# Convolution stage: GpSimd folds four of nine term slots into four others, TensorE sums five, and the low half of the products comes in two pieces

## The chip, the core and the metric

The kernel runs on one core of a Trainium2 chip. The metric is device time in microseconds (us), the median of several executions; lower is better. Five engines work side by side, each in the order of its own queue: TensorE (PE in the profile; PEld is its weight load), VectorE (DVE), ScalarE (ACT), GpSimd (POOL) and SyncE (SP), which only issues DMAs here. They meet through semaphores.

## What is computed

A two-block network on x of 8 x 256 x 512 (batch, rows, columns) with a context of the same shape. The change touches only the first part of the first block, the long convolution:

```
k_ = k.reshape(B, H, head_dim, L)        # k and v are ctx, q is layernorm(x)
kv = jnp.einsum('bhil,bhjl->bijhl', k_, v_)
y = irfft(rfft(kv, n=2 * L) * rfft(ssm_kernel, n=2 * L))[..., :L]
out = y + kv * D
out = jnp.einsum('bijhl,bhil->bjhl', out, q_)
x = x + jnp.tanh(g_xattn[0]) * out
```

with 8 batches, 32 heads, 8 rows per head and L = 512. For each head and each pair (i, j) of rows the product of two context rows is convolved along its 512 columns with the head's filter, weighted with a row of the normalised x, and summed over i. Everything after it (mixture of experts, linear attention, soft mixture of experts) stays as it is.

## The kernel before, in words

The convolution is done by conv_stage (line 141) as multiplication with a Toeplitz matrix. Since k and v are the same tensor, only the 36 pairs with i <= j are made (PAIRS). The stage runs in 16 steps (STEPS, index s) of two heads each, and each step in 4 blocks of 128 columns (KD, index m). Per step:

- VectorE, pairs(s) (lines 340 to 354): the products of context rows, 2304 elements in each of 128 partitions, in f32, as two instructions of 2048 and 256 elements. Both inputs of both lie in SBUF.
- ScalarE, split(s) (line 307): prod_hi, the products rounded to f16.
- GpSimd (line 274): prod_lo, what the rounding left over, also f16, in one instruction.
- TensorE, convolve(s, m) (line 451): for the two heads and the blocks up to m three matmuls each, high by high, high by low and low by high; 6, 12, 18 and 24 matmuls for m = 0 to 3. The result lies in a ring of three PSUM places. It waits for the Toeplitz tile of its step (toep_loaded) and for the low half (lo_done).
- VectorE, weigh(s, m) (lines 380 to 383): four multiplications of the PSUM result with q_e, into the f32 tile terms. Its 72 places of 16 elements are nine slots (SLOTS_T) of 128 elements; 8 results (j) by 16 lie in each slot. terms has three buffers (M_BUFS).
- TensorE, add_up(n) with n = 4s + m (line 468): nine transposes with accumulation in PSUM add up the nine slots and turn them back.
- VectorE, add_rows(s) (line 392): tanh(gate) times the sum, plus x.
- SyncE (lines 253 to 258): the Toeplitz load of step s + 2 (two buffers), 8 stores of step s, 8 loads of x for step s + 2, in this order, in one queue.

TensorE's order is convolve(n), then add_up(n - 2). VectorE's order in step s is weigh(s,0), weigh(s,1), weigh(s,2), add_rows(s-1), pairs(s+2), weigh(s,3) (lines 419 to 431). In steps 1 to 4 further transposes of the second half of the inputs lie between them ("turn", in steps 1 to 4 after m = 1 and m = 3), and in steps 2 and 3 the LayerNorm of the second half ("normalise" and "scale"). weigh(n) waits until add_up(n - 3) has freed its buffer, and convolve(n) until weigh of the unit three places earlier has freed its place in the ring.

Of the kernel before, what the change touches and what calls it, by code (L numbers as in the profile page):

```python
# [14 lines left out]
ALU = mybir.AluOpType  # L15
AX = mybir.AxisListType

P = 128
# [3 lines left out]
KD = D // P  # L22
# [16 lines left out]
def opener(nc, stack):  # L39

    def sb(name, shape, dt=F32):
        return stack.enter_context(nc.sbuf_tensor(name, shape, dt))

    def ps(name, shape, dt=F32):
        return stack.enter_context(nc.psum_tensor(name, shape, dt))

    def sem(name):
        return nc.alloc_semaphore(name)
    return sb, ps, sem
# [68 lines left out]
STEPS = SSM_H // 2  # L118
GSTEPS = STEPS // 2
PAIRED = 2 * B * PAIRS  # L120
SLOTS_T = 9
RUN = 8 * SLOTS_T
WRAP = SSM_I + 4


def spread(a, *dims):

    return bass.AP(tensor=a.tensor, offset=a.offset, ap=[a.ap[0], *([s, n] for s, n in dims)])
# [12 lines left out]
def conv_stage(nc, k, x, ctx, ssm_reversed, ssm_d, g_xattn, g_ffn, ssm_split, x1):  # L141
# [5 lines left out]
    with phase(nc) as st:  # L147
        sb, ps, sem = opener(nc, st)
# [5 lines left out]
        T_BUFS, M_BUFS, RING = 2, 3, 3  # L154
        toep = sb("toep", [P, T_BUFS, 2, 2, D], F16)
        prod = sb("prod", [P, 2, PAIRED * KD])
        prod_hi, prod_lo = (sb(f"prod_{n}", [P, 2, KD, 2, B * PAIRS], F16) for n in ("hi", "lo"))
        terms = sb("terms", [P, M_BUFS, RUN, 2 * B])
# [10 lines left out]
        toep_loaded = [sem(f"toep_loaded{u}") for u in range(T_BUFS)]  # L169
        res_loaded, stored = [sem(f"res_loaded{u}") for u in range(2)], [sem(f"stored{u}") for u in range(2)]  # L170
        prod_done, hi_done, lo_done = sem("prod_done"), sem("prod_hi_done"), sem("prod_lo_done")
        conv_done, weighed, summed, added = sem("conv_done"), sem("weighed"), sem("summed"), sem("x_added")
        block = st.enter_context(nc.Block())

        x_t, c_t = (a.rearrange("b (e g r) d -> g e r b d", e=2, g=2) for a in (x, ctx))
# [44 lines left out]
        @block.sync  # L220
        def _(sp):
            def load(t, g, u):
                for e in range(2):
                    src = (c_t if t == "c" else x_t)[g, e, :, u * 4:u * 4 + 4, :]
                    sp.dma_start(rows[t][e * 64:e * 64 + 64, u * 4:u * 4 + 4, :], src).then_inc(loaded[t][u], 16)

            def load_res(s):
                if s >= 2:
                    sp.wait_ge(added, s - 1)
                for j in range(SSM_I):  # L230
                    sp.dma_start(res[j * 16:j * 16 + 16, s % 2, :], x_s[s, j]).then_inc(res_loaded[s % 2], 16)

            def load_toeplitz(s):
                sp.wait_ge(conv_done, (s - T_BUFS + 1) * KD)
                toeplitz(sp, s)

            def store(s):
                sp.wait_ge(added, s + 1)
                for j in range(SSM_I):
                    sp.dma_start(x1_s[s, j], gated[j * 16:j * 16 + 16, s % 2, :]).then_inc(stored[s % 2], 16)  # L240

            for t in "cq":
                for u in range(2):
                    load(t, 0, u)
            load_res(0)
            load_res(1)
            for u in range(2):
                sp.wait_ge(turned["c"], 2 * u + 2)
                load("c", 1, u)
            for u in range(2):  # L250
                sp.wait_ge(normed, 4 * u + 4)
                load("q", 1, u)
            for s in range(STEPS):
                if s + T_BUFS < STEPS:
                    load_toeplitz(s + T_BUFS)
                store(s)
                if s + 2 < STEPS:
                    load_res(s + 2)
            for u in range(2):
                sp.wait_ge(stored[u], STEPS // 2 * 128)  # L260

        @block.gpsimd
        def _(pool):
            nc.gpsimd.memset(k.ident[:, :], 0.0).then_inc(ident_zeroed, 1)
            pool.wait_ge(ident_zeroed, 1)
            nc.gpsimd.affine_select(out=k.ident[:, :], in_=k.ident[:, :], compare_op=ALU.not_equal, fill=1.0,
                                    base=0, pattern=[[-1, P]], channel_multiplier=1).then_inc(ident_ready, 1)
            nc.gpsimd.memset(terms[:, :, :, :], 0.0).then_inc(zeroed, 1)
            for s in range(STEPS):
                u = s % 2  # L270
                pool.wait_ge(hi_done, s + 1)
                if s >= 2:
                    pool.wait_ge(conv_done, (s - 1) * KD)
                nc.gpsimd.tensor_tensor(prod_lo[:, u].rearrange("p k e r -> p (k e r)"), prod[:, u, :],  # L274
                                        prod_hi[:, u].rearrange("p k e r -> p (k e r)"), ALU.subtract).then_inc(lo_done, 1)

        @block.scalar
        def _(act):
# [49 lines left out]
        def _(dve):  # L328
# [11 lines left out]
            def pairs(s):  # L340

                u = s % 2
                if s >= 2:
                    dve.wait_ge(lo_done, s - 1)
                if s == 0:
                    dve.wait_ge(out_act, 4)
                    dve.wait_ge(out_dve, 4)
                if s == GSTEPS:
                    dve.wait_ge(out_act, turns["c", 1, 3] + 1)
                c = c_e[:, s].rearrange("p k e b i -> p (k e b) i")  # L350
                dst = prod[:, u, :].rearrange("p (r n) -> p r n", n=PAIRS)
                nc.vector.tensor_tensor(spread(dst, (PAIRS, 64), (8, 4), (1, 8)), spread(c, (WRAP, 64), (0, 4), (1, 8)),
                                        spread(c, (WRAP, 64), (1, 4), (1, 8)), ALU.mult)
                nc.vector.tensor_tensor(dst[:, :, 32:PAIRS], c[:, :, 0:4], c[:, :, 4:8], ALU.mult).then_inc(prod_done, 1)
# [79 lines left out]
        @block.tensor  # L434
        def _(pe):
            pe.wait_ge(ident_ready, 1)

            def turn(unit):
                t, g, n = unit
                wait_free(pe, unit)  # L440
                if t == "c":
                    pe.wait_ge(loaded["c"][n // 2], (g + 1) * 32)
                else:
                    pe.wait_ge(normed, g * 8 + n * 2 + 2)
                for half in range(2):
                    for b in range(KD):
                        row = rows["c"][:, 2 * n + half, :] if t == "c" else xn[:, 2 * (n % 2) + half, :]
                        last = nc.tensor.transpose(ring[:, bank(unit), half, b * P:(b + 1) * P], row[:, b * P:(b + 1) * P], k.ident[:, :])
                last.then_inc(turned[t], 1)

            def convolve(s, m):
                unit, u = ("conv", s, m), s % T_BUFS
                wait_free(pe, unit)
                if m == 0:
                    pe.wait_ge(toep_loaded[u], (s // T_BUFS + 1) * 16)
                    pe.wait_ge(lo_done, s + 1)
                for e in range(2):
                    out = ring[:, bank(unit)].rearrange("p h c -> p (h c)")[:, D + (e - 1) * B * PAIRS:D + e * B * PAIRS]
                    for n in range(m + 1):
                        t = D - P - (m - n) * P  # L460
                        w_hi, w_lo = (toep[:, u, e, q, t:t + P] for q in range(2))
                        hi, lo = (a[:, s % 2, n, e, :] for a in (prod_hi, prod_lo))
                        nc.tensor.matmul(out, w_hi, hi, start=(n == 0), stop=False)  # L463
                        nc.tensor.matmul(out, w_hi, lo, start=False, stop=False)  # L464
                        last = nc.tensor.matmul(out, w_lo, hi, start=False, stop=(n == m))  # L465
                last.then_inc(conv_done, 1)

            def add_up(n):

                s, m = divmod(n, KD)  # L470
                pe.wait_ge(weighed, n + 1)
                if m == 0 and s >= 2:
                    pe.wait_ge(added, s - 1)
                out = total[:, s % 2, m * P:(m + 1) * P]
                for o in range(SLOTS_T):
                    last = nc.tensor.matmul(out, terms[:, n % M_BUFS, o * 8:o * 8 + 8].rearrange("p j n -> p (j n)"), k.ident[:, :],
                                            is_transpose=True, start=(o == 0), stop=(o == SLOTS_T - 1))
                last.then_inc(summed, 1)

            for unit in units:  # L480
                if unit[0] != "conv":
                    turn(unit)
                    continue
                convolve(*unit[1:])
                n = unit[1] * KD + unit[2]
                if n >= 2:
                    add_up(n - 2)
            add_up(STEPS * KD - 2)
            add_up(STEPS * KD - 1)


# [1736 lines left out]
```

## Time and profile before

| | us |
|---|---|
| median of three executions | 2036.13 (2035.11 to 2039.6) |
| the profiled execution, whole | 2038.1 |
| its span, first to last instruction | 2036.3 |
| convolution stage, first matmul of step 0 to the end of the last add_rows | 51.1 to 265.0 |

| engine over the whole span | busy us | share |
|---|---|---|
| PE | 1699.5 | 83% |
| DVE | 1141.6 | 56% |
| ACT | 716.2 | 35% |
| POOL | 419.4 | 21% |

All times are counted from the start of the span. A busy PE is not PE at its peak. In brackets behind a row stands how long the engine had been idle before it, and what ended that; "issue" means that the profile shows nothing that it waited for. A DMA's time in the timeline is the time of issuing it, not that of the transfer. A repetition "x9" stands for nine instructions in a row.

### The profile page before, as it was taken

The page shows a single profiled execution, that of the slowest core. Times are in us where ns is not written, and L with a number is a line of the kernel's source. Part 1 is how long each engine was busy: PE and PEld are TensorE (multiplying, and loading weights), DVE is VectorE, ACT ScalarE, POOL GpSimd, SP SyncE. Part 2 cuts the span into 40 slices and gives each one's busy share as a digit, 9 for nine tenths or more (in the row PEclk, how much of TensorE's full clock was granted, in tenths as well). Part 3 has the DMA queues.
Part 4 walks back from the last instruction along what each step waited for, and adds up shares of the span by engine and source line. Part 5 has one row for each costly group of instructions (what it writes and reads, how often), then busy time and mean ns, then how long its engine had stood idle before and what let it go on. Part 6 is the DMA issues. An engine that isn't in the chain of part 4 may idle for free. (4 is left out here: it accounts for less than half of the span.)

```text
span 2036.3 us, 29066 instructions
## 1 busy us (share of the span) xinstructions
PE 1699.5 (83%) x10248; PEld 1006.8 (49%) x10249; DVE 1141.6 (56%) x2234; ACT 716.2 (35%) x1366; POOL 419.4 (21%) x324
## 2 busy tenths in 40 slices
PE   2989948999279999588988736798989898989898
PEld 2778823444146666344544413454545454545454
DVE  4978843332643333576868646646465655556463
ACT  2322113333222222242333225735454443535352
POOL 1323303333411110233222113501010101010100
PEclk6999979999689999789999868899999899999999
DMA  8222233333422222433020052200000000000000
GB/s 179 62 74 86 86 119 107 119 119 99 134 68 84 82 82 68 185 104 103 13 92 21 11 176 66 90 1 32 1 32 0 31 0 31 0 31 0 21 13 20
DMA packets 78734, 134.52 MB, mean 66 GB/s; under 512 B 6626, under 2 KB 31202, under 8 KB 78514
## 3 DMA queue, kind: packets, MB, share of 16 engines
q1 hardware_dynamic: 71488, 113.45, 17.4%
q0 software_dynamic: 5680, 18.62, 3.2%
q10 hardware_dynamic: 1474, 1.21, 0.2%
q8 instruction: 59, 0.97, 0.2%
q14 instruction: 33, 0.27, 0.0%
HBM read 101.98 MB, written 31.28 MB: 65 GB/s over the span
## 5 line engine op out<-in xcount | busy, mean ns | idle before, releaser
L2041 PE MATMUL s_ring<-w_mu_hi,s_xt_hi 128*128 128x512 f16 x256 | 104.7, 409 | 45.7 <-DVE s_xt_lo L1948 45.7
L1953 DVE TENSOR_REDUCE s_top<-s_lg 128x1 f32<-128x512 f32 x64 | 43.8, 685 | 130.5 <-ACT s_lg L1855 130.5
L463 PE MATMUL ring<-prod_hi,toep 128*128 128x288 f16 x320 | 93.0, 291 | 18.2 <-DVE terms L383 10.1
L274 POOL TENSOR_TENSOR prod_lo<-prod,prod_hi 128x2304 f16<-128x2304 f32 x16 | 73.2, 4576 | 166.9 <-ACT prod_hi L307 156.6
L2025 DVE TENSOR_TENSOR s_g_lo<-s_ring,s_g_hi 128x512 f16<-128x512 f32 x64 | 43.4, 689 | 109.9 <-ACT s_g_hi L1897 109.9
L2042 PE MATMUL s_ring<-w_mu_lo,s_xt_hi 128*128 128x512 f16 x256 | 104.4, 408 | 0.0
L2043 PE MATMUL s_ring<-w_mu_hi,s_xt_lo 128*128 128x512 f16 x256 | 103.8, 405 | 0.0
L1800 POOL TENSOR_TENSOR s_h_lo<-s_h,s_h_hi 128x512 f16<-128x512 f32 x32 | 36.9, 1154 | 311.7 <-DVE s_h_hi L2022 311.7
L1794 POOL TENSOR_TENSOR s_xln<-s_xln,s_gamma 128x512 f32<-128x512 f32 x16 | 21.7, 1376 | 372.2 <-DVE s_xln L1934 372.2
L2041 PE MATMUL s_ring<-w_w_hi,s_xt_hi 128*128 128x512 f16 x256 | 98.0, 383 | 0.0
L2042 PE MATMUL s_ring<-w_w_lo,s_xt_hi 128*128 128x512 f16 x256 | 98.0, 383 | 0.0
L2043 PE MATMUL s_ring<-w_w_hi,s_xt_lo 128*128 128x512 f16 x256 | 97.8, 382 | 0.0
L2041 PE MATMUL s_acc<-w_w_hi,s_g_hi 128*128 128x512 f16 x256 | 97.1, 379 | 0.0
L2042 PE MATMUL s_acc<-w_w_lo,s_g_hi 128*128 128x512 f16 x256 | 97.0, 379 | 0.0
L2043 PE MATMUL s_acc<-w_w_hi,s_g_lo 128*128 128x512 f16 x256 | 97.0, 379 | 0.0
L464 PE MATMUL ring<-prod_lo,toep 128*128 128x288 f16 x320 | 93.0, 291 | 0.0
L465 PE MATMUL ring<-prod_hi,toep 128*128 128x288 f16 x320 | 93.0, 290 | 0.0
L2006 DVE TENSOR_TENSOR s_xw_lo<-s_ring,s_xw_hi 128x512 f16<-128x512 f32 x64 | 44.1, 689 | 73.0 <-ACT s_xw_hi L1889 73.0
L1855 ACT ACTIVATE s_lg<-s_ring,s_rs 128x512 f32<-128x512 f32 x64 | 44.0, 688 | 115.8 <-PE s_ring L2043 115.8
L380 DVE TENSOR_TENSOR terms<-ring,q_e 128x512 f32<-128x512 f32 x64 | 66.8, 1044 | 27.3 <-PE ring L465 25.0
L1087 DVE TENSOR_TENSOR e_h<-e_up,e_silu 128x352 f32<-128x352 f32 x39 | 20.4, 524 | 109.3 <-ACT e_silu L1066 109.3
L991 POOL DMA_INDIRECT e_rows<-normed_rows,slot_token x39 | 37.0, 950 | 197.6 <-PE e_turn L1005 181.7
(396 smaller groups left out, 4919.2 us busy)
## 6 DMA issues: line engine op xcount, KB each, us to landing
expert_rows<-e_y SPq DMA_DIRECT2D x39, 256.0 KB, 2.0
toep<-ssm_split SPq DMA_DIRECT2D x14, 512.0 KB, 5.1
stage<-in_L_ffn_gate_w SPq DMA_DIRECT2D x8, 704.0 KB
stage<-in_L_ffn_up_w SPq DMA_DIRECT2D x8, 704.0 KB
c_rows<-in_ctx SPq DMA_DIRECT2D x8, 512.0 KB, 10.3
x_rows<-in_x SPq DMA_DIRECT2D x8, 512.0 KB
res<-in_x SPq DMA_DIRECT2D x128, 32.0 KB
after_conv<-gated SPq DMA_DIRECT2D x128, 32.0 KB
```

The lines of the kernel that those rows point to most:

```text
L274: nc.gpsimd.tensor_tensor(prod_lo[:, u].rearrange("p k e r -> p (k e r)"), prod[:, u, :], prod_hi[:, u].rearrange("p k e r -> p (k e r)"), ...
L380: nc.vector.tensor_tensor(to(0, (9, 4), (1, 8)), values(0, (8, 4), (1, 8)), weights(0, (0, 4), (1, 8)), ALU.mult)
L463: nc.tensor.matmul(out, w_hi, hi, start=(n == 0), stop=False)
L464: nc.tensor.matmul(out, w_hi, lo, start=False, stop=False)
L465: last = nc.tensor.matmul(out, w_lo, hi, start=False, stop=(n == m))
L1855: A(lg[:, t, j * D:(j + 1) * D], ring[:, bank, :], ACT.Copy, scale=rs[:, t:t + 1]).then_inc(S["lg_out"], 1)
L1953: V.tensor_reduce(top[:, t, j:j + 1], lg[:, t, j * D:(j + 1) * D], AX.X, ALU.max).then_inc(S["top_done"], 1)
L2006: V.tensor_tensor(xw[1][:, t, j * D:(j + 1) * D], ring[:, bank, :], xw[0][:, t, j * D:(j + 1) * D], ALU.subtract).then_inc(S["xw_lo"], 1)
L2025: V.tensor_tensor(g[1][:, n % G_BUFS, :], ring[:, bank, :], g[0][:, n % G_BUFS, :], ALU.subtract).then_inc(S["g_lo"], 1)
L2041: mm(out_, a[0], b_[0], start=first, stop=False)
L2042: mm(out_, a[0], b_[1], start=False, stop=False)
L2043: return mm(out_, a[1], b_[0], start=False, stop=last_)
```

## The change

GpSimd, which made only prod_lo before, gets a fold for each of the 64 pairs (s, m): one addition of 128 x 512 f32 that adds slots 0 to 3 of terms to slots 5 to 8, in place. TensorE then sums slots 4 to 8, five transposes in place of nine, and waits for the fold (folded) where it waited for weigh (weighed). prod_lo of step s + 1 is made in two pieces of 1152 elements. GpSimd's queue in step s is low_half(s+1,0), fold(s,0), fold(s,1), low_half(s+1,1), fold(s,2), fold(s,3). The counts of lo_done double. The ring place is still freed by weighed, the buffer of terms by summed.

```diff
--- before.py
+++ after.py
@@ -118,7 +118,7 @@
 STEPS = SSM_H // 2
 GSTEPS = STEPS // 2
 PAIRED = 2 * B * PAIRS
-SLOTS_T = 9
+SLOTS_T, FOLDED = 9, 5
 RUN = 8 * SLOTS_T
 WRAP = SSM_I + 4
 
@@ -169,7 +169,7 @@
         toep_loaded = [sem(f"toep_loaded{u}") for u in range(T_BUFS)]
         res_loaded, stored = [sem(f"res_loaded{u}") for u in range(2)], [sem(f"stored{u}") for u in range(2)]
         prod_done, hi_done, lo_done = sem("prod_done"), sem("prod_hi_done"), sem("prod_lo_done")
-        conv_done, weighed, summed, added = sem("conv_done"), sem("weighed"), sem("summed"), sem("x_added")
+        conv_done, weighed, folded, summed, added = sem("conv_done"), sem("weighed"), sem("folded"), sem("summed"), sem("x_added")
         block = st.enter_context(nc.Block())
 
         x_t, c_t = (a.rearrange("b (e g r) d -> g e r b d", e=2, g=2) for a in (x, ctx))
@@ -266,13 +266,28 @@
             nc.gpsimd.affine_select(out=k.ident[:, :], in_=k.ident[:, :], compare_op=ALU.not_equal, fill=1.0,
                                     base=0, pattern=[[-1, P]], channel_multiplier=1).then_inc(ident_ready, 1)
             nc.gpsimd.memset(terms[:, :, :, :], 0.0).then_inc(zeroed, 1)
-            for s in range(STEPS):
-                u = s % 2
+
+            def low_half(s, half):
+                u, ks = s % 2, slice(half * 2, half * 2 + 2)
                 pool.wait_ge(hi_done, s + 1)
                 if s >= 2:
                     pool.wait_ge(conv_done, (s - 1) * KD)
-                nc.gpsimd.tensor_tensor(prod_lo[:, u].rearrange("p k e r -> p (k e r)"), prod[:, u, :],
-                                        prod_hi[:, u].rearrange("p k e r -> p (k e r)"), ALU.subtract).then_inc(lo_done, 1)
+                nc.gpsimd.tensor_tensor(prod_lo[:, u, ks].rearrange("p k e r -> p (k e r)"),
+                                        prod[:, u, half * 2 * PAIRED:(half + 1) * 2 * PAIRED],
+                                        prod_hi[:, u, ks].rearrange("p k e r -> p (k e r)"), ALU.subtract).then_inc(lo_done, 1)
+
+            def fold(n):
+                t = terms[:, n % M_BUFS].rearrange("p f n -> p (f n)")
+                pool.wait_ge(weighed, n + 1)
+                nc.gpsimd.tensor_tensor(t[:, 5 * P:9 * P], t[:, 5 * P:9 * P], t[:, 0:4 * P], ALU.add).then_inc(folded, 1)
+
+            low_half(0, 0)
+            low_half(0, 1)
+            for s in range(STEPS):
+                for m in range(KD):
+                    if m % 2 == 0 and s + 1 < STEPS:
+                        low_half(s + 1, m // 2)
+                    fold(s * KD + m)
 
         @block.scalar
         def _(act):
@@ -341,7 +356,7 @@
 
                 u = s % 2
                 if s >= 2:
-                    dve.wait_ge(lo_done, s - 1)
+                    dve.wait_ge(lo_done, 2 * (s - 1))
                 if s == 0:
                     dve.wait_ge(out_act, 4)
                     dve.wait_ge(out_dve, 4)
@@ -453,7 +468,7 @@
                 wait_free(pe, unit)
                 if m == 0:
                     pe.wait_ge(toep_loaded[u], (s // T_BUFS + 1) * 16)
-                    pe.wait_ge(lo_done, s + 1)
+                    pe.wait_ge(lo_done, 2 * (s + 1))
                 for e in range(2):
                     out = ring[:, bank(unit)].rearrange("p h c -> p (h c)")[:, D + (e - 1) * B * PAIRS:D + e * B * PAIRS]
                     for n in range(m + 1):
@@ -468,13 +483,13 @@
             def add_up(n):
 
                 s, m = divmod(n, KD)
-                pe.wait_ge(weighed, n + 1)
+                pe.wait_ge(folded, n + 1)
                 if m == 0 and s >= 2:
                     pe.wait_ge(added, s - 1)
                 out = total[:, s % 2, m * P:(m + 1) * P]
-                for o in range(SLOTS_T):
+                for o in range(SLOTS_T - FOLDED, SLOTS_T):
                     last = nc.tensor.matmul(out, terms[:, n % M_BUFS, o * 8:o * 8 + 8].rearrange("p j n -> p (j n)"), k.ident[:, :],
-                                            is_transpose=True, start=(o == 0), stop=(o == SLOTS_T - 1))
+                                            is_transpose=True, start=(o == SLOTS_T - FOLDED), stop=(o == SLOTS_T - 1))
                 last.then_inc(summed, 1)
 
             for unit in units:
```

## Rows read from the trace of the kernel before

**Rows 1.** Busy time by stretch: from:to, length, engines with counts, granted clock, DMA share, GB/s.

```profile
128.38:250.50 122.12, 114.41 (x961) 98.14 (x962) 104.61 (x191) 22.41 (x14) 45.81 (x10) 1.00 0.27 87
...
94.57:97.98 3.41, 3.41 (x15) 2.43 (x16) 3.41 (x8) 0.24 (x1) 3.09 (x1) 0.50 0.14 46
```

**Rows 2.** Timeline of TensorE: start, duration, instruction; an add_up, then conv(s,0).

```profile
187.65 1.15 PE L476 MATMUL rows_total<-ident,terms 128*128 128x128 f32 x9
189.61 0.28 PE L463 MATMUL ring<-prod_hi,toep 128*128 128x288 f16 x1 [0.82 <-issue]
```

**Rows 3.** Timeline of SyncE's issues over one step.

```profile
174.26 4.90 SPq L240 DMA_DIRECT2D after_conv<-gated  x8
179.21 5.20 SPq L231 DMA_DIRECT2D res<-in_x  x8
184.45 0.41 SPq L218 DMA_DIRECT2D toep<-ssm_split  x1
```

**Rows 4.** Page: two GpSimd groups (busy, mean ns), then an issue with time to landing.

```profile
L274 POOL TENSOR_TENSOR prod_lo<-prod,prod_hi 128x2304 f16<-128x2304 f32 x16 | 73.2, 4576 | 166.9 <-ACT prod_hi L307 156.6
...
L1800 POOL TENSOR_TENSOR s_h_lo<-s_h,s_h_hi 128x512 f16<-128x512 f32 x32 | 36.9, 1154 | 311.7 <-DVE s_h_hi L2022 311.7
...
toep<-ssm_split SPq DMA_DIRECT2D x14, 512.0 KB, 5.1
```

**Rows 5.** Timeline of VectorE: pairs in two neighbouring steps.

```profile
174.16 2.28 DVE L352 TENSOR_TENSOR prod<-c_e 128x2048 f32<-128x2048 f32 x1
...
186.38 2.27 DVE L352 TENSOR_TENSOR prod<-c_e 128x2048 f32<-128x2048 f32 x1
```

**Rows 6.** Timeline of GpSimd between these two.

```profile
179.01 4.58 POOL L274 TENSOR_TENSOR prod_lo<-prod,prod_hi 128x2304 f16<-128x2304 f32 x1 [7.66 <-ACT prod_hi L307]
```

**Rows 7.** Timeline of VectorE and GpSimd where two of their instructions meet.

```profile
55.06 4.58 POOL L274 TENSOR_TENSOR prod_lo<-prod,prod_hi 128x2304 f16<-128x2304 f32 x1 [16.55 <-ACT prod_hi L307]
...
58.74 3.05 DVE L352 TENSOR_TENSOR prod<-c_e 128x2048 f32<-128x2048 f32 x1
61.72 0.41 DVE L354 TENSOR_TENSOR prod<-c_e 128x256 f32<-128x256 f32 x1
62.05 1.06 DVE L380 TENSOR_TENSOR terms<-ring,q_e 128x512 f32<-128x512 f32 x1
...
63.74 0.26 DVE L383 TENSOR_TENSOR terms<-ring,q_e 128x64 f32<-128x64 f32 x1
...
551.97 1.48 DVE L926 TENSOR_TENSOR behind<-slot_f,edges 128x1280 f16<-128x1280 f32 x1
551.98 2.48 POOL L842 TENSOR_TENSOR w_down_lo<-d_stage,w_down_hi 96x512 f16<-96x512 f32 x1
```

**Rows 8.** Single lines: ns least/median/most, first and last start, shapes.

```profile
L94 DVE TENSOR_TENSOR x_mean<-x_stats x12: 158/166/4381, 34.1 to 1067.7; 128x4 f32<-128x4 f32 x12
...
L842 POOL TENSOR_TENSOR w_down_lo<-d_stage,w_down_hi x6: 1147/1150/2478, 535.6 to 552.0; 96x512 f16<-96x512 f32 x6
...
L380 DVE TENSOR_TENSOR terms<-ring,q_e x64: 1006/1042/1075, 53.2 to 261.0; 128x512 f32<-128x512 f32 x64
...
L699 DVE SCALAR_TENSOR_TENSOR h<-gu,bu,silu x24: 741/751/752, 313.7 to 503.0; 128x512 f32<-128x512 f32 x20, 64x512 f32<-64x512 f32 x4
...
L1797 POOL TENSOR_TENSOR s_xln<-s_xln,s_beta x16: 1258/1266/1442, 1217.3 to 1899.5; 128x512 f32<-128x512 f32 x16
```

**Rows 9.** Timeline of a later stage: VectorE waits while two GpSimd instructions stand queued.

```profile
1214.63 2.65 POOL L1794 TENSOR_TENSOR s_xln<-s_xln,s_gamma 128x512 f32<-128x512 f32 x2 [36.83 <-DVE s_xln L1934]
1216.29 1.28 DVE L1909 TENSOR_SCALAR s_dt<-s_dt 128x512 f32<-128x512 f32 x1 [1.35 <-ACT s_dt L1824]
1217.25 2.66 POOL L1797 TENSOR_TENSOR s_xln<-s_xln,s_beta 128x512 f32<-128x512 f32 x2
```

**Rows 10.** Timeline of TensorE: a longer idle in step 3.

```profile
94.52 0.41 PE L463 MATMUL ring<-prod_hi,toep 128*128 128x288 f16 x1 [2.09 <-DVE terms L383]
```

**Rows 11.** Timeline: the first VectorE instruction of the stage after.

```profile
279.56 2.47 DVE L83 BATCH_NORM_STATS2 x_stats<-x_in 128x6 f32<-128x512 f32 x4 [14.59 <-DMA x_in<-after_conv]
```

## The prediction

> **What bounds the convolution now.** I read four views in this order: busy time by stretch, SyncE's issues, the three compute engines over one step, and GpSimd. The share of busy time misleads. From the first matmul of step 5 to that of step 15 TensorE is busy 114.41 of 122.12 us [rows 1], which looks like the bound, and one step takes 12.21 us. But in every step it idles 0.8 us in front of conv(s,0), with "issue" as releaser [rows 2]. The issue list explains it: SyncE issues the Toeplitz tile at 184.45, such a load lands 5.1 us after its issue (the median), and conv starts at 189.61 [rows 2 to 4]. SyncE is late with that load because it first issues 8 stores (4.90 us) and 8 residual loads (5.20 us), which begin when add_rows ends [rows 3]. So a loop over two steps sets the pace: add_rows done, 10.2 us of issues, 5.1 us landing, 0.1 us to conv(s,0), and from there to the end of add_rows(s-1) the 9.0 us that are left of two steps (24.4). (Check: the stores begin at 174.26, released by an add_rows that has just ended; 4.90 and 5.20 us of issues later the tile is issued at 184.45.) VectorE is nearly as full, 104.61 of the same 122.12 us, and GpSimd works 45.81 of them: one instruction of 4.58 us per step [rows 1, 6], then rest.
>
> **What the change removes.** Four of nine transposes per add_up. Nine take 1.15 us of which 0.27 is the last one's own length, so one is (1.15-0.27)/8 = 0.11 us [rows 2] and an add_up gets 0.44 us shorter, 1.76 us per step, 28 us over 64 add_ups. On the path lies little of it: between conv(s,0) and weigh(s,2) stand two add_ups, 0.88 us, and this counts once in a loop of two steps. If nothing else changed, a step would be 0.44 us shorter.
>
> **What it adds.** 64 folds on GpSimd, 128x512 f32 plus f32 into f32. The nearest row is the same form in a later stage, line 1797 with a least of 1.26 us [rows 8]; bounds are 1.15 us (line 1800, f16 out) [rows 4] and 1.44 (the most of line 1797, which had to wait for VectorE) [rows 8]. I take 1.26, since only that row has f32 out. A GpSimd instruction queued behind another starts 0.03 to 0.04 us before that one ends [rows 9], so it advances the queue by 1.22. The halves of the low part have 1152 elements: between 512 (1.15 us) and 2304 (4.58) the slope is 1.91 ns [rows 4], which gives 2.38 us, or 2.34 in a queue; the two together are 4.76, against 4.58 undivided. GpSimd then has 4 x 1.26 + 4.76 = 9.8 us per step. That alone would fit in 12.2.
>
> **Why it does not fit.** It is not alone. pairs is a VectorE tensor_tensor with both inputs in SBUF. At 58.74 it met a running GpSimd instruction (55.06 to 59.65): it took 3.05 us instead of 2.28, and the next one began at 61.72, 2.07 us after GpSimd's end [rows 7]. A 128x4 addition of two SBUF inputs (line 94), 0.17 us as a median, took 4.38 at most [rows 8]. The other way round, GpSimd's line 842 began at 551.98 beneath a VectorE instruction of that kind and took 2.48 us [rows 7], where its least is 1.15 [rows 8]. They take turns, a whole instruction at a time. Instructions with one input in PSUM don't: weigh stays within 1.01 to 1.08 us, and line 699 (PSUM, SBUF and a column, the form of add_rows) at 0.74 to 0.75, although GpSimd runs beside both [rows 8]. The Trainium skill has this as a rule, in "SBUF — State Buffer", section "Who interferes with whom": a VectorE instruction with two SBUF inputs and a GpSimd instruction that reads SBUF share one port pair as an exclusive lock. By a reading in which both merely slow each other, the change would be the gain of the first rival below; by this rule it is a loss, and the trace agrees with the rule.
>
> The before kernel hardly met this: its one GpSimd instruction (179.01 to 183.59) lay between two pairs (174.16 and 186.38) [rows 5, 6]. With the change GpSimd works through a queue of six, and pairs must fall into it. Put zero at the end of low_half(s+1,1). pairs(s+2) and fold(s,2) both stand ready. If VectorE goes first:
> - 0 to 2.40: pairs(s+2), 2.07 + 0.33 [rows 7]. fold(s,2) waits, then runs 2.40 to 3.66.
> - 2.40 to 4.35: weigh(s,3), 1.95 us from its first start to its last end [rows 7]; 0.07 to hand over.
> - 4.42: fold(s,3) 1.22, low_half(s+2,0) 2.34, fold(s+1,0) 1.22, fold(s+1,1) 1.22, low_half(s+2,1) 2.38; this ends at 12.80, where pairs(s+3) begins.
>
> This is a closed loop: **12.80 us** per step against 12.21, plus 0.59. Is anything else later? TensorE runs conv(s+1,0) from about 1.2 to 1.9 (Toeplitz landing), waits for fold(s,2) until 3.75, then add_up, conv(s+1,1), fold(s,3) at 5.7, conv(s+1,2) until 8.6; weigh(s+1,2) and add_rows end by 11.4. So pairs(s+3) stands ready 1.4 us ahead of the lock, and the saved transposes buy nothing: TensorE's saving turns into a wait.
>
> **Sum for the convolution.** Steps 5 to 13, eight intervals in the new loop: 8 x 0.59 = +4.7. Steps 0 to 4: with the same durations carried through by hand add_rows(0) comes 2.7 us later (pairs(2) waits for fold(1), prod_lo and fold(2) for pairs); in steps 2 and 3 VectorE waits for the LayerNorm's transposes anyway, and 1.6 of it vanish there: +1.1 (bounds 0 and 3). Steps 14 and 15 have no pairs; the loop's 2.40 us falls away, of which 1.7 come back before the Toeplitz landing is the later one: -1.7. At the end fold(63) stands between the last weigh and its add_up: 1.26 + 0.07 - 0.44 = +0.9. Together +5.0.
>
> **The clock.** TensorE now idles 1.9 us in each step before add_up(s,2). Before, an idle of 2.09 us ahead of 94.52 [rows 10] was followed by a granted clock of 0.50 for 3.41 us, and the ten steps with 0.8 us of idle stayed at 1.00, the 2.4 GHz level [rows 1]. I expect about half of the ten steady steps to get such a stretch at 1.2 GHz. It stretches 3.4 us of TensorE's time by at most 1.7, of which the 1.4 us of cushion before pairs hides most: 0.5 us each, +2.5; bounds 0 and 14 (eight steps at 1.7).
>
> Sum: +5.0 + 2.5 = +7.5. The profiled execution took 2038.1 us (span 2036.3, 1.8 around it), 2 us above the median of the three runs, 2036.1; the stage after begins with 14.59 us of VectorE's idle until a DMA [rows 11] and takes the shift as it is. So 2045.6 for an execution like the profiled one, **2043.6** as a median.
>
> **Rivals.**
> 1. *No turn-taking that matters; faster.* If folds slipped in beside pairs, the two-step loop of before would hold, with 0.88 us out of it: -0.44 x 10 steps, -1 to -2 in the early steps, +0.9 for the tail: -5, 2031. Against it stand the three cases of blocking [rows 7, 8]. It decides once the blocking adds less than those 0.44 us per step to the loop. Chance 0.08.
> 2. *GpSimd goes first.* fold(s,2) has been ready since weigh(s,2), pairs only after add_rows, 0.7 us later. If the earlier one wins, fold(s,2) precedes pairs and the loop is 12.80 + 1.22 = 14.02: 8 x 1.22 = +9.8, +2 in the early steps, 2055. Against it: at 1216.29 a VectorE instruction waited beneath GpSimd's line 1794 while line 1797 stood ready; VectorE ended at 1217.57, 0.3 us after line 1794 (1214.63 + 2.65), and the first of line 1797, begun at 1217.25, took 1.44 us instead of 1.26 [rows 8, 9]. Chance 0.12. The same section of the skill says that issue order decides who blocks; by that rule this rival would come true, and the rows of this case speak for VectorE.
> 3. *Dearer folds or a clock that falls in nearly every step.* Folds of 1.44 add 3 x 0.18 x 8 = 4.3; the clock's bound adds 11: 2048 to 2055. Chance 0.20.
> 4. *Lost in the noise.* Folds of 1.15, no clock change, and no loss in the early steps: 5.0 - 1.1 - 3 x 0.11 x 8 = +1.3, 2037; up to +4. Chance 0.17.
> My forecast, 2040 to 2048, has 0.43.
>
> **How the numbers follow.** This kernel's measurement can tell 0.2%, 4.1 us, from no change. Faster is rival 1, 0.08. Within: rival 4, 0.17. Slower: the rest, 0.75. The range leaves out rival 1 and the top of rivals 2 and 3: 2036 to 2056.
>
> **What would show it.** Right: pairs (its first instruction) at 3 to 4 us instead of 2.28, starting while a low half runs; fold(s,2) with a length of over 3 us because it waits; add_rows 12.7 to 12.9 apart; an idle of about 2 us of TensorE before add_up(s,2), released by GpSimd; the Toeplitz wait still there. Wrong: pairs at 2.28 (rival 1), or pairs beginning its work only after fold(s,2), add_rows 14 apart (rival 2). If folds are over 1.4 us even where no pairs is near, the term was mis-sized. If add_rows are below 12.2 apart, the loop is not the bound and the prediction falls.

## The result, and the profile after

| | us |
|---|---|
| median after | 2057.89 (2056.25 to 2060.93, 4 runs) |
| median before, beside it | 2037.87 (2035.11 to 2039.68, 4 runs) |
| ratio | 1.0095, 95% interval 1.0069 to 1.0121 |
| predicted | 2043.6, range 2036.0 to 2056.0 |
| span of the profiled execution, before and after | 2036.3, 2056.9 |

The change makes the kernel 20 us slower. The direction was forecast, the size was not: 7.5 us were expected, and the time lies 1.9 us above the range. By the spans 20.6 us were lost, 13.1 more than expected.

Where the 20.6 us of the two spans come from, read off the starts of add_rows in the two timelines: add_rows(5) begins 7.3 us later (156.29 against 148.99), the eight intervals up to add_rows(13) add 13.5 (267.47 against 246.65, so 13.90 us per step against 12.21), the last two steps give 1.1 back (the last add_rows ends at 284.66 against 264.97), and everything behind the convolution adds 0.9.

Busy time by stretch after, from the first matmul of step 5 to that of step 15 (columns as in [rows 1]):

```profile
133.31:270.31 137.00, 101.98 (x802) 79.17 (x800) 126.71 (x191) 22.76 (x14) 114.13 (x60) 1.00 0.25 77
```

TensorE now works 101.98 of 137.00 us, where it had 114.41 of 122.12 [rows 1]. VectorE shows 126.71, although it computes the same as before in its 104.61: 22 us of its "busy" time are instructions that stand and wait. GpSimd went from 45.81 to 114.13. A busy share does not tell work from waiting inside an instruction; the lengths do. VectorE and GpSimd over one step (start, duration; they answer to [rows 5, 6]):

```profile
183.98 2.37 POOL L275 TENSOR_TENSOR prod_lo<-prod,prod_hi 128x1152 f16<-128x1152 f32 x1
186.31 3.31 POOL L282 TENSOR_TENSOR terms<-terms 128x512 f32<-128x512 f32 x1
191.84 1.28 POOL L282 TENSOR_TENSOR terms<-terms 128x512 f32<-128x512 f32 x1 [2.21 <-DVE terms L398]
193.07 2.38 POOL L275 TENSOR_TENSOR prod_lo<-prod,prod_hi 128x1152 f16<-128x1152 f32 x1
195.41 2.51 POOL L282 TENSOR_TENSOR terms<-terms 128x512 f32<-128x512 f32 x2
197.86 2.39 POOL L275 TENSOR_TENSOR prod_lo<-prod,prod_hi 128x1152 f16<-128x1152 f32 x1
...
184.07 0.75 DVE L407 SCALAR_TENSOR_TENSOR gated<-rows_total,tanh_gates,res 128x512 f32<-128x512 f32 x1
184.73 3.77 DVE L367 TENSOR_TENSOR prod<-c_e 128x2048 f32<-128x2048 f32 x1
188.42 1.48 DVE L369 TENSOR_TENSOR prod<-c_e 128x256 f32<-128x256 f32 x1
189.83 1.04 DVE L395 TENSOR_TENSOR terms<-ring,q_e 128x512 f32<-128x512 f32 x1
...
197.99 0.73 DVE L407 SCALAR_TENSOR_TENSOR gated<-rows_total,tanh_gates,res 128x512 f32<-128x512 f32 x1
```

Read it in the order of the ends. The low half ends at 186.35. The first instruction of pairs (L367), which stood there since 184.73, now computes and ends at 188.50. The fold (L282) that began at 186.31 ends at 189.62: it waited beneath pairs and then had its 1.2 us. The second instruction of pairs (L369) takes 1.48 us in place of 0.41: it stood beneath that fold. So the fold was computed **between the two instructions of pairs**. Only then comes weigh (L395) at 189.83, and behind it the next fold, after 2.21 us of GpSimd's idle. And TensorE:

```profile
189.68 0.77 PE L491 MATMUL rows_total<-ident,terms 128*128 128x128 f32 x5 [1.85 <-POOL terms L282]
```

It waits 1.85 us for the fold, then sums five slots.

### The profile page after: what moved, and what is told of

Read it like the earlier page. It is cut to its first block and busy times, and to the rows that moved or that the text cites. A ratio compares the mean times of both kernels' runs of the same rounds, so it can differ in the third digit from the quotient of the medians.

```text
span 2056.9 us, 28648 instructions
## 1 busy us (share of the span) xinstructions
PE 1681.1 (82%) x9992; PEld 979.9 (48%) x9993; DVE 1168.8 (57%) x2234; ACT 716.9 (35%) x1366; POOL 523.2 (25%) x404
## 3 DMA queue, kind: packets, MB, share of 16 engines
HBM read 101.98 MB, written 31.28 MB: 65 GB/s over the span
## 5 line engine op out<-in xcount | busy, mean ns | idle before, releaser
L282 POOL TENSOR_TENSOR terms<-terms 128x512 f32<-128x512 f32 x64 | 103.6, 1627 | 55.2 <-DVE terms L398 55.1
L275 POOL TENSOR_TENSOR prod_lo<-prod,prod_hi 128x1152 f16<-128x1152 f32 x32 | 76.5, 2392 | 45.8 <-ACT prod_hi L322 45.8
## 6 DMA issues: line engine op xcount, KB each, us to landing
x_rows<-in_x SPq DMA_DIRECT2D x8, 512.0 KB, 13.3
```

Source lines behind the costliest of these rows:

```text
L275: nc.gpsimd.tensor_tensor(prod_lo[:, u, ks].rearrange("p k e r -> p (k e r)"), prod[:, u, half * 2 * PAIRED:(half + 1) * 2 * PAIRED], prod ...
L282: nc.gpsimd.tensor_tensor(t[:, 5 * P:9 * P], t[:, 5 * P:9 * P], t[:, 0:4 * P], ALU.add).then_inc(folded, 1)
```

## The experiments

In what follows, add_rows "13.9 apart" means the time from the start of one add_rows to that of the next, and a stretch at half clock is one with a granted clock of 0.50.

Theory A, formed from the profile after: VectorE instructions with two SBUF inputs and GpSimd instructions that read SBUF take turns, whole instructions, **in the order in which they arrive**, and an engine arrives when its previous instruction has ended, not when the semaphores of the next are satisfied. The second instruction of pairs arrives later than the queued fold, so the fold gets in between. The loop is then 2.07 + 1.2 + 0.33 (pairs with a fold in it), 1.95 (weigh(s,3)), 0.07 (handover) and 8.38 (the queue behind it: three folds and two low halves, 3 x 1.22 + 2.34 + 2.38): 14.0 us, measured 13.9 between add_rows. Its rivals were a GpSimd that is simply full, a loop through TensorE, the granted clock, and the loop through SyncE that I had read from the profile before.

### The fold out of the middle of pairs

```diff
             def fold(n):
                 pool.wait_ge(weighed, n + 1)
+                if n % KD == 2 and n // KD + 2 < STEPS:
+                    pool.wait_ge(prod_done, n // KD + 3)
```

> The changed kernel, but fold(s,2) also waits until both instructions of pairs(s+2) are done; GpSimd and VectorE have the same work as before. Theory A (turns in order of arrival: GpSimd arrives at the shared port only when its previous instruction ends, and gets its turn between the two instructions of pairs): this alone takes one fold, 1.2 us, out of the loop. The second instruction of pairs falls from 1.48 to 0.41 us, add_rows come 12.8 us apart in steps 5 to 13 instead of 13.9, and the whole takes 2044 to 2049. Rival B (GpSimd is simply full, and the folds' place does not matter): GpSimd does the same work and one fold even later, add_rows stay 13.9 apart, 2058 or more. Rival C (the granted clock): no difference, 2058.

Measured: 2053.28 against 2036.67 beside it, ratio 1.008 (1.0063 to 1.0097). The mechanism is as theory A says: the second instruction is back at 0.41 (once, in step 0, a low half got in: 2.59), and the fold waits for it:

```profile
L371 DVE TENSOR_TENSOR prod<-c_e x16: 410/414/2587, 31.4 to 252.4; 128x256 f32<-128x256 f32 x16
...
198.35 0.41 DVE L371 TENSOR_TENSOR prod<-c_e 128x256 f32<-128x256 f32 x1
...
198.91 1.28 POOL L284 TENSOR_TENSOR terms<-terms 128x512 f32<-128x512 f32 x1 [2.63 <-DVE prod L371]
```

The time missed the forecast of 2044 to 2049: by the two spans (2053.4 and 2056.9) it gained 3.5 us over the changed kernel and not 9 to 14, and the intervals of the two ratios overlap, so that the gain shows in the steps and not in the whole time. Add_rows came 12.8 apart from step 5 to 6, but 14.3 once, 13.5 in five later steps, 11.8 in the last, and 13.3 in the mean of eight. Each of the steps of 14.3 and 13.5 has a stretch of 3.41 us at half clock, which the changed kernel does not have there:

```profile
125.30:173.00 47.70, 38.71 (x310) 30.71 (x308) 42.25 (x67) 10.52 (x12) 33.63 (x21) 1.00 0.27 84
173.05:176.46 3.41, 2.99 (x13) 2.27 (x14) 2.55 (x7) 1.09 (x1) 2.92 (x3) 0.50 0.13 51
```

In the five steps of 13.5 the first instruction of pairs took 2.55 to 2.57 us (2.28 alone [rows 5]), so it hardly waited for GpSimd: there the loop of theory A was no longer what set the pace. Rival B (13.9 whatever the order) is out, and so is rival C, since the changed kernel has a clock of 1.00 in these steps. Without half clock were two steps, those of 12.8 and 11.8. That the clock (which I had priced at 0.5 us for such a step) took back the 0.7 us of the others goes by this coincidence; no run here holds the clock fixed.

### Another order in GpSimd's queue

```diff
                 for m in range(KD):
-                    if m % 2 == 0 and s + 1 < STEPS:
+                    if m in (0, 3) and s + 1 < STEPS:
                         low_half(s + 1, m // 2)
                     fold(s * KD + m)
```

> The changed kernel with two entries of GpSimd's queue exchanged: low_half(s+1,0), fold(s,0), fold(s,1), fold(s,2), low_half(s+1,1), fold(s,3). The work is the same. Theory A (turns by arrival, and GpSimd arrives when its previous instruction ends): fold(s,2) arrives before pairs, so the first instruction of pairs waits only 0.5 to 0.7 us for it (about 2.9 us long), but the low half arrives next and gets its turn between the two instructions of pairs, so the second one takes 2.6 to 2.8 us instead of 1.48; GpSimd rests longer before fold(s,2), and add_rows come 14.1 to 14.5 apart. Rival M (only the sum of GpSimd's work and pairs counts, or pairs is let through as one): second instruction of pairs 0.41 us or 1.48 as before, add_rows 12.8 to 13.9 apart.

Measured: 2070.90, in a single execution. With fold(s,2) ahead of the low half, the low half is what is queued when pairs begins, and it goes in between:

```profile
L367 DVE TENSOR_TENSOR prod<-c_e x16: 2276/2958/2970, 29.1 to 269.4; 128x2048 f32<-128x2048 f32 x16
...
L369 DVE TENSOR_TENSOR prod<-c_e x16: 414/2578/2583, 31.4 to 272.3; 128x256 f32<-128x256 f32 x16
...
194.21 2.95 DVE L367 TENSOR_TENSOR prod<-c_e 128x2048 f32<-128x2048 f32 x1
197.08 2.58 DVE L369 TENSOR_TENSOR prod<-c_e 128x256 f32<-128x256 f32 x1
...
193.75 1.27 POOL L282 TENSOR_TENSOR terms<-terms 128x512 f32<-128x512 f32 x1 [1.22 <-DVE terms L398]
194.98 4.40 POOL L275 TENSOR_TENSOR prod_lo<-prod,prod_hi 128x1152 f16<-128x1152 f32 x1
```

The two instructions of pairs take 2.96 and 2.58 us, the low half 4.40 in place of 2.38. Of the eight steps two were 14.2 us long, as expected, and the other six 14.9 to 16.0; the mean is 14.9, above the 14.1 to 14.5 expected, with eight stretches at half clock from step 5 on. With the same work the last add_rows ends 16.9 us later than in the changed kernel; the part behind the convolution gives 4.7 of them back, which leaves 12.2 in the span. Rival M is out. Add_rows(5) comes 7.9 us later than there, with little more time at half clock up to it (31 against 27 us) and with 2.58 us for the second instruction of pairs in five passes, where the changed kernel had 1.48 or 1.49 in two of them and 0.41 in three. The next eight steps add 8.2 us: 0.3 per step goes with the order alone (14.2 against 13.9), and the rest came together with the stretches at half clock.

### A fold that only writes

```diff
-                nc.gpsimd.tensor_tensor(t[:, 5 * P:9 * P], t[:, 5 * P:9 * P], t[:, 0:4 * P], ALU.add).then_inc(folded, 1)
+                nc.gpsimd.memset(t, 0.0).then_inc(folded, 1)
```

> The changed kernel with a memset of 1152 elements of the same buffer in the place of each fold (GpSimd only writes, about 1 us; the sum is then zero). Theory A in the form that only GpSimd instructions that read SBUF take turns with pairs: pairs waits for the low half, but the memset runs beside it: second instruction of pairs 0.41 us, add_rows 12.2 to 12.6 apart. Form A2 (any GpSimd instruction takes its turn): second instruction of pairs about 1.2 us, add_rows 13.1 or more apart. Rival B: 13.9 less four times 0.2, 13.1.

Measured: 2048.96 in a single execution, add_rows 12.6 apart in the mean of eight, 11.1 to 14.0 by turns; the three steps of 13.7 to 14.0 have a stretch at half clock each.

```profile
165.54 2.33 DVE L367 TENSOR_TENSOR prod<-c_e 128x2048 f32<-128x2048 f32 x1
165.65 1.07 POOL L282 MEMSET terms<- 128x1152 f32 x1
167.79 0.41 DVE L369 TENSOR_TENSOR prod<-c_e 128x256 f32<-128x256 f32 x1
```

The memset runs beside pairs: it takes 1.07 us (1.06 where nothing else runs), and pairs 2.33 and 0.41. Form A2 is out: this GpSimd instruction, which reads nothing, took no turn. That agrees with the Trainium skill, "SBUF — State Buffer", section "Who interferes with whom", by which a VectorE instruction with two SBUF inputs contends with a GpSimd instruction that reads SBUF and not with one that only writes it.

### One size changed: folds of two slots

```diff
-SLOTS_T, FOLDED = 9, 5
+SLOTS_T, FOLDED = 9, 7
...
-                nc.gpsimd.tensor_tensor(t[:, 5 * P:9 * P], t[:, 5 * P:9 * P], t[:, 0:4 * P], ALU.add).then_inc(folded, 1)
+                nc.gpsimd.tensor_tensor(t[:, 7 * P:9 * P], t[:, 7 * P:9 * P], t[:, 0:2 * P], ALU.add).then_inc(folded, 1)
```

> The changed kernel with one size changed: each fold adds two slots to two others (256 elements) and TensorE sums seven. Theory A gives a formula for the closed loop of GpSimd and VectorE: pairs 2.40 + weigh 1.95 + 0.07 + low pieces 4.72 + four folds. With folds of 1.22 that is 14.0 (measured 13.9); a fold of 256 elements takes about 0.67 us and advances the queue by 0.63, so the loop is 11.7, shorter than the 12.2 us of the loop through SyncE. So add_rows come 12.1 to 12.5 apart, and the whole takes 2034 to 2041. Rival J (what costs is that a fold stands between weigh and the sum at all, not its length): 13 or more apart, 2048 or more.

Measured: 2038.87 against 2037.39, ratio 1.000 (0.9982 to 1.0018), and the steps are 12.22 us apart, the kernel before's 12.21.

```profile
L282 POOL TENSOR_TENSOR terms<-terms x64: 721/728/2775, 57.3 to 266.9; 128x256 f32<-128x256 f32 x64
```

A fold of 256 takes 0.73 us; in the formula (0.69 in a queue) the closed loop is 11.9, so the loop through SyncE is the longer one again; in the trace conv(s,0) starts 0.09 us after the landing of its Toeplitz tile in every step from 6 on. Rival J is out: the length of the folds costs, not their place behind weigh. It also says where the price of folding begins in this kernel: as long as the closed loop stays below 12.2 us folding costs nothing, and it brings nothing.

### All nine transposes back

```diff
-SLOTS_T, FOLDED = 9, 5
+SLOTS_T, FOLDED = 9, 9
```

> The changed kernel, but TensorE transposes all nine slots again behind the fold (four slots are then in the sum twice). Theory A: GpSimd and VectorE close the loop, TensorE has cushion: add_rows 13.9 apart as in the changed kernel, the whole 2057 to 2062. Rival E (the folds stand in TensorE's way, and the loop runs through TensorE): 0.44 to 1.76 us more per step, 2064 to 2078.

Measured: 2062.37 in a single execution. Add_rows 13.9 apart in every step from 6 to 13, as in the changed kernel; the last add_rows ends 6.2 us later than there, of which 4.2 are lost up to add_rows(5) and the rest in the last two steps, and the span is 3.7 us longer. In the steady part the 28 us of transposes are worth nothing beside the folds, as predicted.

### The gain without the price: no folds

```diff
                 for m in range(KD):
                     if m % 2 == 0 and s + 1 < STEPS:
                         low_half(s + 1, m // 2)
-                    fold(s * KD + m)
+                    pass
...
-                pe.wait_ge(folded, n + 1)
+                pe.wait_ge(weighed, n + 1)
```

> The changed kernel without the folds: TensorE sums five of nine slots right behind weigh, so four slots are left out of the sum. The low half stays in two pieces. This is the gain of the change without its price. Theory A (in the kernel before, SyncE's loop over two steps sets the pace, so that the 1.76 us that TensorE saves per step count only 0.44): add_rows 11.8 to 11.9 apart, conv(s,0) still starts 0.1 us after the Toeplitz tile lands, 2027 to 2031. Rival D (TensorE was the bound before, as its busy share says): 12.2 - 1.76 = 10.5 apart, 2010 or so.

Measured: 2042.74 in a single execution, no faster than before; both forecasts were wrong. The last add_rows ends at 268.1, 3 us later than before. From step 5 to 15:

```profile
126.58:255.37 128.79, 104.65 (x802) 85.10 (x800) 105.80 (x194) 22.76 (x14) 47.19 (x20) 0.93 0.26 82
```

Steps are 10.4 to 16.5 us apart by turns, and conv(s,0) starts 0.09 us after the landing of its tile in each of them from step 6 on: the loop through SyncE is confirmed as the limit. But two terms that I had kept fixed moved. The tile lands after a median of 5.8 us in place of 5.1 (7.0 to 7.2 in three steps, where SyncE had issued the stores and loads before it without a rest since the tile before), and there are four stretches at half clock (mean 0.93 in this window, 1.00 before [rows 1]). What each of the two cost is not separated here.

### The Toeplitz load out of SyncE's queue

```diff
             for s in range(STEPS):
-                if s + T_BUFS < STEPS:
-                    load_toeplitz(s + T_BUFS)
                 store(s)
...
                 if s + 2 < STEPS:
+                    act.wait_ge(conv_done, (s + 1) * KD)
+                    toeplitz(act, s + 2)
                     split(s + 2)
```

On the kernel before:

> The kernel before, with one edit: the Toeplitz tile of step s+2 is issued from ScalarE's queue, in front of split(s+2) and behind the same wait (all of step s convolved), in the place of SyncE's queue. Theory A (SyncE's 16 issues make the tile late, and a loop over two steps through them sets the pace): conv(s,0) no longer starts 0.1 us after the landing, the next limit is TensorE with 60 x 0.1225 + 36 x 0.11 = 11.3 us per step, ten steps save 0.9 each, 2025 to 2030. Rival F (the idle in front of conv(s,0) has another cause, or ScalarE's issue delays split as much): 12.2 apart, 2036.

Measured: 2033.59 against 2035.92, ratio 0.9982 (0.9968 to 0.9997).

```profile
128.39:241.19 112.80, 112.80 (x962) 98.43 (x960) 103.21 (x189) 22.78 (x14) 45.87 (x10) 1.00 0.28 90
...
259.68 0.75 DVE L392 SCALAR_TENSOR_TENSOR gated<-rows_total,tanh_gates,res 128x512 f32<-128x512 f32 x1 [6.05 <-DMA res<-in_x]
```

Ten steps take 112.80 us, 11.28 each as forecast, with TensorE busy all the time. Rival F is out. But of the 9 us only 4.5 reach the end of the stage, since the last add_rows waits 6.05 us for its load of x, and 2 the total. That load had come nearer with every step: the last of the loads of x landed 7.0 us before add_rows(5), 2.2 before add_rows(10) and 0.08 before add_rows(12).

On the changed kernel the same edit does nothing:

> The changed kernel with the Toeplitz load on ScalarE's queue as well. Theory A (in the changed kernel the closed loop of GpSimd and VectorE is later than the tile): add_rows stay 13.9 apart, 2055 to 2060. Rival H (the loop through SyncE still counts in the changed kernel): about 0.9 less per step, 2049 or less.

Measured: 2057.03 in a single execution, add_rows 13.9 apart. There SyncE has ceased to matter; rival H is out.

On the run without folds:

> The run without folds (five of nine slots summed, four left out) and the Toeplitz load on ScalarE's queue. It tells why leaving out 28 us of transposes did not pay in the run without folds. Theory A (the late tile was the limit, and its landing grew as the loop got shorter): with the load out of SyncE's queue TensorE needs 9.5 us per step and VectorE 10.35, add_rows 10.4 to 11.0 apart, 2015 to 2024. Rival G (stretches at half clock eat the saving, since TensorE is less busy): add_rows 11.3 or more apart and more stretches at 0.50 than the kernel before has, 2026 or more.

Measured: 2033.08 in a single execution. The first two intervals are 10.4 us, as theory A has it, then it goes to 11.8, with add_rows waiting 1.3 us:

```profile
203.51 0.75 DVE L407 SCALAR_TENSOR_TENSOR gated<-rows_total,tanh_gates,res 128x512 f32<-128x512 f32 x1 [1.34 <-issue]
...
193.44 6.28 SPq L240 DMA_DIRECT2D after_conv<-gated  x8
199.76 5.47 SPq L231 DMA_DIRECT2D res<-in_x  x8
205.28 6.26 SPq L240 DMA_DIRECT2D after_conv<-gated  x8
```

There is one stretch at half clock in that part (the forecast of rival G was several), so the clock is not it. The landing times in the trace say what is: in every step from 7 on the last of the loads of x landed 0.08 us before add_rows began, while the stores whose buffer it overwrites had landed 5 us or more before. SyncE has no rest any more: 8 stores (6.28 us) and 8 loads (5.47 us) fill the 11.8 us of a step. So the limit was still behind SyncE's queue, now by the loads of x in place of the tile. Whether SyncE's issues or the transfers set that pace this run does not tell. A measured 11.8 is between the two forecasts.

### SyncE only stores

To the Toeplitz load on ScalarE's queue comes:

```diff
-                if s + 2 < STEPS:
-                    load_res(s + 2)
...
                 if s + 2 < STEPS:
                     act.wait_ge(conv_done, (s + 1) * KD)
                     toeplitz(act, s + 2)
                     split(s + 2)
+                if 1 <= s < STEPS - 1:
+                    act.wait_ge(added, s)
+                    for j in range(SSM_I):
+                        act.dma_start(res[j * 16:j * 16 + 16, (s + 1) % 2, :], x_s[s + 1, j]).then_inc(res_loaded[(s + 1) % 2], 16)
```

> The kernel before with the Toeplitz loads and the loads of x for add_rows on ScalarE's queue (the latter behind split), so that SyncE only stores. With the Toeplitz loads alone the steps were 11.3 apart, but the last add_rows waited 6.05 us for its load of x. Theory A: SyncE's queue is the limit at both places; steps 11.3 apart, no wait in front of the last add_rows, convolution done at 255 to 257 instead of 265, the whole 2026 to 2029. Rival K (16 more issues per two steps delay ScalarE's split, which the steps wait for): 11.8 or more apart, 2032 or more.

Measured: 2034.60 against 2037.39, ratio 0.998 (0.9961 to 0.9998). Steps 11.3 apart up to step 11, as expected, then 11.9, and the end at 261.7 and not 256: the last add_rows again waits, 4.98 us. As with the Toeplitz load alone moved, the loads of x land 0.08 us before add_rows from step 12 on.

```profile
toep<-ssm_split ACTq DMA_DIRECT2D x9, 512.0 KB, 10.1
...
260.95 0.75 DVE L394 SCALAR_TENSOR_TENSOR gated<-rows_total,tanh_gates,res 128x512 f32<-128x512 f32 x1 [4.98 <-issue]
...
217.19 40.41 SPq L240 DMA_DIRECT2D after_conv<-gated  x32
```

The landing of the tile grew from 5.1 us to a median of 10.1 in this stretch. The issues grew too: SyncE, which now only stores, took 40.41 us for 32 stores, 1.26 us each, where it had 0.61 [rows 3]. That speaks for the transfers as what falls behind, not the engine that issues them. Why, I did not settle: no run here separates the number of the transfers from their bytes. With folds of two slots behind pairs added on top:

> Folds of two slots, fold(s,2) behind pairs(s+2), seven transposes, and both kinds of loads on ScalarE's queue. Theory A: TensorE needs 11.3 - 0.9 = 10.4 us per step, VectorE 10.35, GpSimd 7.3, so without SyncE in the way folding pays at last: 10.4 to 11.2 apart, 2018 to 2027, below the run with the loads alone. Rival L (turns and waits between VectorE and GpSimd, or stretches at half clock, take the 0.9 us back): 11.3 or more apart, 2027 or more.

Measured: 2036.51, ratio 0.9995 (0.9975 to 1.0015), steps 11.5 apart. Folding does not pay even there, and of rival L it is the waits that hold: from step 6 to 12 the clock is 1.00, and the tile and the loads of x land in time. With the fold behind pairs a chain runs through three engines: fold(s,2) waits for pairs (GpSimd idle 2.9 us per step), TensorE waits 0.8 to 1.0 us for that fold, weigh(s+1,2) 1.0 us for TensorE, and the next pairs stands behind it and add_rows.

### The low half in two pieces alone

```diff
-                nc.gpsimd.tensor_tensor(prod_lo[:, u].rearrange("p k e r -> p (k e r)"), prod[:, u, :],
-                                        prod_hi[:, u].rearrange("p k e r -> p (k e r)"), ALU.subtract).then_inc(lo_done, 1)
+                for half in range(2):
+                    ks = slice(half * 2, half * 2 + 2)
+                    nc.gpsimd.tensor_tensor(prod_lo[:, u, ks].rearrange("p k e r -> p (k e r)"),
+                                            prod[:, u, half * 2 * PAIRED:(half + 1) * 2 * PAIRED],
+                                            prod_hi[:, u, ks].rearrange("p k e r -> p (k e r)"), ALU.subtract).then_inc(lo_done, 1)
```

> The kernel before with only the low half in two pieces, one right behind the other. Theory A (GpSimd has 7.7 us of rest per step there, and the two pieces cost 0.1 to 0.2 us more than one): nothing, add_rows 12.2 apart, 2034 to 2040. Rival I (a piece more on GpSimd meets pairs by itself): 0.3 us or more per step, 2040 or more.

Measured: 2038.79 in a single execution; intervals of 12.1 to 12.3 in all steps from 4 on but two (12.8 and 13.1). This part of the change costs nothing that these runs can tell.

## Why the prediction was right in its direction and wrong in its size

- **What bounds the kernel before: right.** The idle named "issue" in front of conv(s,0) was the Toeplitz tile, and SyncE's issues made it late. With the load on another queue the steps fell to 11.28 us.
- **What the removed transposes are worth: right that it is next to nothing, wrong as a number.** I credited 0.44 us per step if nothing else changed; without folds the kernel was 2042.74. The step took the tile's landing and the clock as fixed, and both got worse; which of them ate the gain is open.
- **Lengths of the new instructions: right.** Folds 1.28 (1.26 forecast), low halves 2.38 (2.38).
- **Blocking between pairs and GpSimd: right**, and it is what costs.
- **"0 to 2.40: pairs(s+2). fold(s,2) waits, then runs 2.40 to 3.66": this step failed.** I treated the two instructions of pairs as one turn. The fold had stood waiting since 186.31, before the second of them began at 188.42, and was served first. That puts 1.2 us into every pass of the loop: 14.0 by the same sum, 13.9 measured, in place of 12.80. Over eight intervals it is 8.8 of the 13.1 us that I missed. The others are 6.2 in the early steps, 0.9 behind the convolution, 2.5 that I gave to the clock and that did not come there, and 0.3 too much for the last two steps (8.8 + 6.2 + 0.9 - 2.5 - 0.3 = 13.1).
- **Rival 2 had this price** (14.02 per step, 2055) **and the wrong picture**: I asked only whether the fold would come before pairs or after it. The row of line 1909 had settled that rightly; it was one VectorE instruction and could not tell what happens between two. [rows 7] had the answer within reach: the step from 58.74 to 62.05 shows no GpSimd instruction queued behind the one that ended, so its 2.07 + 0.33 could not be carried over. As to the Trainium skill's rule that issue order decides who blocks ("SBUF — State Buffer", section "Who interferes with whom"), the trace agrees if an instruction counts as issued once nothing of its own engine stands in front of it: the fold was ready since weigh(s,2), but stood in front only at 186.31.
- **Steps 0 to 4: too small.** +1.1 forecast, +7.3 at add_rows(5). add_rows(0) came 2.5 us late, near the 2.7 forecast, and add_rows(1) 4.8. The 1.6 us that were to vanish in steps 2 and 3 did not: add_rows(2) was 4.6 late and add_rows(3) 6.4. Part of it is the same failed step: in three of the six passes up to add_rows(5) the second instruction of pairs took 1.48 or 1.49 us in place of 0.41, at most 3.2 us together. The rest goes together with four stretches at half clock (27 us in all, 6.8 before); that they cause it is not shown. The run with memsets, with 17 us of them, had add_rows(5) 1.9 us late, the one with nine transposes, also with 17 us, 11.5.
- **The clock: misplaced.** I put 2.5 us on the steady steps; there the clock stayed at 1.00 from 125 us on in spite of 1.85 us of idle per step, and fell in the early steps. In the first experiment it did fall in the steady steps. Where it falls I could not foresee from the profile.
- **The last two steps and the tail: right**, -0.8 forecast, -1.1 measured.

## What to carry to other kernels

Before work is given to GpSimd, list the VectorE instructions with two SBUF inputs and ask of each what GpSimd will have queued when it starts: a queue of GpSimd instructions that read SBUF can get a turn in front of each of them, also between two that stand back to back. Price the closed loop of both engines, not GpSimd's share of busy time. And when an idle is called "issue", look for the landing of a DMA at its end before crediting the engine's work as the bound: 28 us of TensorE's work were taken away here, and nothing was gained even where the folds were left out.

## What the runs showed of the hardware

- Turns between VectorE instructions with two SBUF inputs and GpSimd instructions that read SBUF went by arrival: a fold (1.2 us) or a low half (2.4 us) ran between two adjacent VectorE instructions, which made the second take 1.48 or 2.58 us in place of 0.41.
- A GpSimd memset of 1152 f32 took 1.06 us and did not lengthen the VectorE instructions with two SBUF inputs beside it (2.33 and 0.41 us; 2.28 and 0.41 alone).
- The landing of a 512 KB load is not a constant: 5.1 us in the kernel before, 5.8 without folds, 10.1 when 16 stores and loads per step were issued from two queues at a quicker pace. Nor is the time of issuing a store: 0.61 us in the kernel before, 0.78 where SyncE's queue had no rest (6.28 for 8), 1.26 in the run in which SyncE only stores.
